# Landing-paced indirect transfers in the first mixture-of-experts layers, with two batches' places computed earlier in the order

## The reference

```python
x = x + gated_attention(layernorm(x))        # groups of 32, cumulative state
x = x + ffn(layernorm(x))                    # "first FFN", same weights as the last
x = x + softmax_attention(layernorm(x))      # 16 heads of 64
x = x + ffn(layernorm(x))

def ffn(x):                                  # E=8 experts, K=2, per batch b
    probs = softmax(x @ Wr); p, e = top_k(probs, 2)
    pos = exclusive_cumsum(one_hot(e))       # place of a token in its expert's queue
    keep = pos < capacity                    # capacity = 160
    buf[e, pos] += x * keep                  # scatter: 2048 rows of 128 into 1280 slots
    y = relu(buf @ W1 + b1) @ W2 + b2        # 128 -> 512 -> 128 by expert
    out = sum_k(y[e, pos] * keep * p)        # gather: two rows for each token
```

## Time and profile before

| | us |
|---|---|
| median of 3 runs | 1488.44 |
| lowest, highest run | 1484.74, 1492.68 |
| span of the profiled execution | 1486.9 |
| busy in it: PE, DVE, ACT, POOL | 1437.6, 1065.3, 917.8, 280.4 |

### The profile page before, as it was taken

How to read it: one execution, slowest core, us unless ns; L and a number is a source line. 1 busy time by engine, 2 the same in 40 slices (tenths; PEclk the granted TensorE clock), 3 DMA queues, 4 the chain that set the end, 5 groups by cost and what they waited for, 6 DMA issues and landing times.

```text
span 1486.9 us, 43341 instructions
## 1 busy us (share of the span) xinstructions
PE 1437.6 (97%) x18426; PEld 1023.7 (69%) x18426; DVE 1065.3 (72%) x2172; ACT 917.8 (62%) x1727; POOL 280.4 (19%) x325
## 2 busy tenths in 40 slices
PE   7999789999999999999999999999999999999996
PEld 6988774566677675667777756577777565677486
DVE  6884037888666678886766788876666887787754
ACT  5774466666666666566666666666666666666542
POOL 4164613013210012130000120400001214000055
PEclk9999999999999999999999999999999999999999
DMA  8501221001110011010000110110101101101002
GB/s 223 196 20 53 68 65 39 22 23 46 30 29 16 16 42 32 23 48 16 17 16 16 41 32 22 35 33 17 30 16 39 32 23 34 34 16 30 1 19 58
DMA packets 44464, 58.30 MB, mean 39 GB/s; under 512 B 8231, under 2 KB 32656, under 8 KB 44144
## 3 DMA queue, kind: packets, MB, share of 16 engines
q1 hardware_dynamic: 35120, 38.27, 9.4%
q0 software_dynamic: 9152, 17.26, 4.4%
HBM read 22.14 MB, written 19.32 MB: 28 GB/s over the span
## 4 chain that ended last, share of the span: by engine, by line
PE 87%; DVE 5%; ACT 3%; issue 2%; another core or an unknown queue 2%; DMA 0%; DVEq 0%; ACTq 0%
PE bank L1153 29%; PE bank L1166 28%; PE bank L1076 6%; PE bank L1081 4%; PE bank L1090 4%; PE bank L412 2%; PE bank L446 2%; PE bank L1308 2%; PE bank L1304 2%; DVE nmx L1188 1%; PE bank L1265 1%; ACT hT L542 1%; PE bank L830 1%; DVE stats L1349 1%
## 5 line engine op out<-in xcount | busy, mean ns | idle before, releaser
L1197 ACT ACTIVATE prob<-bank,nmx 128x1024 f32<-128x1024 f32 x512 | 570.2, 1114 | 420.3 <-DVE nmx L1188 408.5
L1188 DVE TENSOR_REDUCE nmx<-bank 128x1 f32<-128x1024 f32 x512 | 626.2, 1223 | 200.2 <-PE bank L1153 182.3
L1166 PE MATMUL bank<-prob,vsc 64*64 64x512 f32 x4096 | 644.9, 590 | 1.9 <-DVE ctxT L1215 1.4
L1153 PE MATMUL bank<-q,k 64*64 64x512 f32 x2048 | 527.6, 591 | 3.1 <-ACT prob L1197 1.9
L1153 PE MATMUL bank<-q,ks 64*64 64x512 f32 x2048 | 526.3, 590 | 0.0
L1166 PEld LDWEIGHTS bank<-prob,vsc 64*64 64x64 f32 x4096 | 237.3, 133 | 119.4 <-issue 47.1
L1076 PE MATMUL bank<-xT,wqkv_sb 64*64 64x256 f32 (+1 forms) x1560 | 211.7, 434 | 0.0
L1153 PEld LDWEIGHTS bank<-q,ks 64*64 64x64 f32 x2048 | 139.1, 133 | 75.9 <-issue 21.0
L1760 POOL DMA_INDIRECT yg<-yslots,row_ring x64 | 64.9, 1014 | 609.2 <-PE bank L1153 579.8
L1153 PEld LDWEIGHTS bank<-q,k 64*64 64x64 f32 x2048 | 135.3, 133 | 37.6 <-issue 8.6
L1076 PEld LDWEIGHTS bank<-xT,wqkv_sb 64*64 64x64 f32 x1560 | 92.2, 133 | 86.6 <-issue 36.5
(11 more groups left out here) (270 smaller groups left out, 1628.6 us busy)
## 6 DMA issues: line engine op xcount, KB each, us to landing
ks<-k SPq DMA_DIRECT2D x62, 256.0 KB
yslots<-slots_sb SPq DMA_DIRECT2D x7, 640.0 KB, 3.6
slots_sb<-xslots SPq DMA_DIRECT2D x5, 640.0 KB, 4.5
xslots<-xhat_r POOLq DMA_DIRECT2D x5, 512.0 KB, 7.0
yslots<-xhat_r POOLq DMA_DIRECT2D x5, 512.0 KB, 12.3
w_sb<-in_w SPq DMA_DIRECT2D x1, 2048.0 KB, 9.2
wqkv_sb<-in_wqkv SPq DMA_DIRECT2D x1, 2048.0 KB, 19.0
xslots<-xhat_r,row_s POOLq DMA_INDIRECT x112
```

The costliest lines, as they stand in the source:

```text
L1153: ins = nc.tensor.matmul(bank[rows(c), SC[h][n], :], kk[r, cols(2 * j + c, HD)], qst[pi % 2][r, cols(n, HALF)], start=True, stop=True)
L1166: ins = nc.tensor.matmul(bank[rows(h), CX[n], :], vsc[s][rows(r), rows(h)], prob[g % 3][h][rows(r), cols(n, HALF)], start=(j == 0 and firs ...
L1188: nc.vector.tensor_reduce(nmx[:, 2 * s + h:2 * s + h + 1], bank[:, SC[h][0]:SC[h][0] + 2, :], mybir.AxisListType.XY, ALU.max, negate=True) ...
L1197: nc.scalar.activation(prob[g % 3][h][:].rearrange("p (n c) -> p n c", c=HALF), bank[:, SC[h][0]:SC[h][0] + 2, :], ACT.Exp, bias=nmx[:, 2 ...
```

## The change

It does five things, all of them within the first FFNs of batches 0, 1 and 2.

1. The waits on TensorE ahead of the scatters and the gathers (`scatter_in_attention`, `scatter_in_next`, `beside_expert`) are gone. In their place each transfer, from the third of a batch on, waits until the one two in front of it has landed. For this every batch has two semaphores of its own, for even and odd transfers, and so have the gathers.
2. GpSimd's list: 12 scatters of batch 0, the bias of row 3, the places of batch 1 (`place_gpsimd(2)`), the other 4 scatters of batch 0, 16 of batch 1, 16 of batch 2, 16 gathers.
3. The slot numbers of batch 1 get a buffer of their own, row_s2, so `place_gpsimd(2)` doesn't wait for scatters.
4. The counting of batch 2's places (`positions(pe, 3, ...)`) stands ahead of the first expert of batch 0's FFN, no longer behind its third; the wait on its reading (f_kept) stands at expert 2, no longer at expert 5.
5. VectorE writes batch 2's slot numbers itself, as the last step of `place_vector`, once batch 0's scatters have landed; GpSimd's copy (L2065) is gone.

```diff
@@ experts_tensor.up
-                if e == 5 and m == 1:
+                if e == 2 and m == 1:
                     pe.wait_ge(f_kept, 3)
@@ first_batch_tensor.beside
-                if e == 3:
-                    positions(pe, 3, POS_F)
                 if e == E - 1:
-                    pe.wait_ge(f_kept, 3)
                     slots_ahead_tensor(pe, 2, slots2, AHEAD[:2])
@@ place_gpsimd
-            if m > 1:
-                p.wait_ge(f_sc, 256 * (m - 1))
-            nc.gpsimd.tensor_copy(row_s[:], skip[:]).then_inc(f_idx, 1)
+            nc.gpsimd.tensor_copy(rows_to(m)[:], skip[:]).then_inc(f_idx, 1)
@@ place_vector
-            nc.vector.tensor_tensor(skip[:], rowf[:], skip[:], ALU.add).then_inc(f_plc, 1)
+            for done in f_sc[1]:
+                v.wait_ge(done, 128)
+            nc.vector.tensor_tensor(rows_to(m)[:], rowf[:], skip[:], ALU.add).then_inc(f_idx, 1)
@@ scatter
             for c in tiles:
                 k, t = c // T, c % T
+                if c > 1:
+                    hold(p, f_sc[m][c % 2], 16 * (c // 2))
                 nc.gpsimd.indirect_dma_start(...)
@@ gather
-                    beside_expert(p, 11 + 2 * q + k)
                     for t in (2 * q, 2 * q + 1):
+                        n = 4 * q + 2 * k + t % 2
+                        if n > 1:
+                            hold(p, f_gq[(n - 2) // 4][n % 2], 16 * ((n - 2) % 4 // 2 + 1))
                         nc.gpsimd.indirect_dma_start(...)
@@ block.gpsimd
             place_gpsimd(p, step, 1)
-            scatter_in_attention(p, 1, 3)
-            scatter_in_next(p, 1)
+            hold(p, f_idx, 2)
+            scatter(p, 1, range(FIRST))          # FIRST = 12
+            bias_gpsimd(p, 3)
             place_gpsimd(p, step, 2)
-            scatter_in_attention(p, 2)
-            scatter(p, 2, [13, 14, 15])
-            p.wait_ge(f_plc, 1)
-            p.wait_ge(f_sc, 256 * 2)
-            nc.gpsimd.tensor_copy(row_s[:], skip[:]).then_inc(f_idx, 1)
+            scatter(p, 1, range(FIRST, 2 * T))
+            hold(p, f_idx, 3)
+            scatter(p, 2, range(2 * T))
             hold(p, f_idx, 4)
-            for i in range(8):
-                beside_expert(p, 3 + i)
-                scatter(p, 3, [2 * i, 2 * i + 1])
+            scatter(p, 3, range(2 * T))
             gather(p, step, 1, 0)
@@ block.tensor
             pe.wait_ge(f_sub, 4)
+            positions(pe, 3, POS_F)
             experts_tensor(pe, 1, first_batch_tensor(pe), (a_res, 10), following=slots2)
```

More of the change, by code:

```diff
@@ L132, in bass_hybrid @@
         f_kept = sem("f_kept")
-        f_plc = sem("f_plc")
         f_xs, f_ha, f_ya, f_ys = (sem(n) for n in ("f_xs", "f_ha", "f_ya", "f_ys"))
-        f_sc, f_ld, f_st, f_comb = (sem(n) for n in ("f_sc", "f_ld", "f_st", "f_comb"))
+        f_sc = {m: [sem(f"f_sc{m}{i}") for i in range(2)] for m in (1, 2, 3)}
+        f_ld, f_st, f_comb = (sem(n) for n in ("f_ld", "f_st", "f_comb"))
         f_ga = [sem("f_ga0"), sem("f_ga1")]
-        f_gq = [sem(f"f_gq{q}") for q in range(4)]
+        f_gq = [[sem(f"f_gq{q}{i}") for i in range(2)] for q in range(4)]
         f_gb = [sem("f_gb0"), sem("f_gb1")]
@@ L271, in route_norm_scalar @@
             elif k == 2:
-                a.wait_ge(f_sc, 256)
+                for done in f_sc[1]:
+                    a.wait_ge(done, 128)
             for half in range(2):
@@ L615, in kept_vector, with rows_to @@
             nc.vector.tensor_scalar(tmp[:], pos, float(CAP - 1), None, ALU.min).then_inc(f_kept, 1)
+        def rows_to(m):
+            return row_s2 if m == 2 else row_s
         def place_gpsimd(p, step, m):
@@ L656, in first_answers_vector @@
             for q in range(4):
-                v.wait_ge(f_gq[q], 64)
+                for done in f_gq[q]:
+                    v.wait_ge(done, 32)
                 for k in range(2):
@@ L669, in scatter @@
                 k, t = c // T, c % T
-                nc.gpsimd.indirect_dma_start(out=xslots[:, :], out_offset=bass.IndirectOffsetOnAxis(ap=row_s[:, k, t:t + 1], axis=0),
+                if c > 1:
+                    hold(p, f_sc[m][c % 2], 16 * (c // 2))
+                nc.gpsimd.indirect_dma_start(out=xslots[:, :], out_offset=bass.IndirectOffsetOnAxis(ap=rows_to(m)[:, k, t:t + 1], axis=0),
                                              in_=route_rows(m - 1)[:, t, :], in_offset=None,
-                                             bounds_check=B * SLOTS - 1, oob_is_err=False).then_inc(f_sc, 16)
-        def scatter_in_attention(p, m, next_row=None):
-            r = m + 2
-            hold(p, f_idx, m + 1)
-            hold(p, a_vproj, 4 * r + 4)
-            scatter(p, m, [0])
-            hold(p, a_lktr, 2 * r + 2)
-            scatter(p, m, [1])
-            hold(p, a_sq, 2 * r + 2)
-            scatter(p, m, [2])
-            for h in range(2):
-                hold(p, a_sl, 2 * r + h + 1)
-                scatter(p, m, [3 + h])
-            for k in range(2):
-                hold(p, a_kv, 4 * r + 2 * k + 1)
-                scatter(p, m, [5 + k])
-            for k in range(4):
-                hold(p, a_o, 4 * r + k + 1)
-                scatter(p, m, [7 + k])
-                if k == 1 and next_row is not None:
-                    bias_gpsimd(p, next_row)
-            for h in range(2):
-                hold(p, a_out, 2 * r + h + 1)
-                scatter(p, m, [11 + h])
-        def scatter_in_next(p, m):
-            r = m + 3
-            hold(p, a_xproj, 2 * r + 2)
-            scatter(p, m, [13])
-            for k in range(2):
-                hold(p, a_gproj, 4 * r + 2 * k + 2)
-                scatter(p, m, [14 + k])
-        def beside_expert(p, i):
-            hold(p, f_h, E + i + 1)
+                                             bounds_check=B * SLOTS - 1, oob_is_err=False).then_inc(f_sc[m][c % 2], 16)
+        FIRST = 12
         def gather(p, step, m, b):
@@ L1415, in f_norm_vector @@
                 else:
-                    v.wait_ge(f_sc, 256 * (B - 1))
+                    for done in f_sc[B - 1]:
+                        v.wait_ge(done, 128)
                 xhat_vector(v, c0, fb, xhat_r, piece - 5, g_xhat)
@@ L1992, in _ @@
                     store_slots(sp, 1, 0)
-                hold(sp, f_sc, 256 * m)
+                for done in f_sc[m]:
+                    hold(sp, done, 128)
                 hold(sp, f_ld, 16 * m)
```

6 lines of the change are left out of this document (4 added, 2 removed).

## The result

| first comparison, 12 runs each | us |
|---|---|
| before, median (lowest, highest) | 1489.7 (1484.74, 1492.68) |
| after, median (lowest, highest) | 1496.32 (1492.65, 1501.3) |
| after / before, 95% interval | 1.0053 (1.0039 to 1.0068) |
| span of the profiled execution after | 1499.5 |

What follows compares the result with a forecast made beforehand. Late TensorE signals were taken as the bound: 20.1 us to gain, but GpSimd's list then binds, leaving the first projection 13.5 earlier, less 1.5 for the clock: 12.0 off, median 1476.4 us, range 1467 to 1487.

Steps and rivals of the forecast that it cites:

- TensorE's signals: Results arriving 3 to 8 us late in dense transfer runs; without these delays TensorE is ready for batch 0's norm 20.1 earlier.
- The first handover: TensorE's passage from batch 0 to batch 1: 6.6 us without late signals, third expert at 161.0 against 167.16, gain 6.2.
- held back in part: Rival: transfer pairs still delay results passed on at once, costing 10 of the 20.1 us; 1481 us, chance 0.18.
- the third of three scatters starts about 3.0 us behind the first: GpSimd's list with landing waits: 2.2 us landing plus 0.86 restart, so the pitch goes from 1.29 to 1.5 us.
- the 1.5 us that the prediction took off for the clock: Loss from TensorE's steps at half the clock after about 6 us idle, before the first projection.
- The rule of the Trainium skill: GpSimd transfer takes 2.0 us plus bytes at 436 GB/s: 2.15 us for 64 KB, so waits would hold nothing.
- the waits hold nothing: Rival: GpSimd's pitch stays 1.29 us, signals come through anyway, TensorE is the bound; 20.1 off, 1468 us, chance 0.12.
- The cover of 0.9 us ahead of batch 2's slots: Batch 2's slots loaded at 168.6, TensorE wanting them at 169.5; if late, TensorE would stall there instead of at the norm.
- if TensorE waits for batch 2's slots and VectorE's norm in turn: Sign of being wrong; the forecast had a single idle stretch, of about 6 us, ahead of batch 0's norm.
- The slower rival: Rival: 52 transfers in one dense run keep holding back TensorE's signals; 20 us slower, 1508 us, chance 0.17.
- a pitch of 1.5: Spacing of GpSimd's paced scatters, between 1.29 us, which held the signals, and 1.56, which didn't; said to decide the slower case.
- hidden today: GpSimd's transfer list, off the bound before the change, becomes the bound: TensorE ready at 191.8 waits for the norm until 199.

Runs made afterwards that it cites:

- e12: The changed kernel without landing waits between scatters or gathers, on chip 10, where late signals appear: 1524.9 us (one run).
- r1: The kernel before, unchanged, profiled a second time on a chip without late signals: 1463.9 us.
- e6: The changed kernel without landing waits and with row 3's bias behind the eighth scatter: 1457.8 us, 0.9963 of the kernel before.
- r2: The changed kernel, unchanged, on a chip without late signals: 1486.0 us, 1.0156 of the kernel before.

## Why the prediction was wrong

**TensorE's signals: right, for the chip of the first comparison.** The first handover took 6.4 us for 6.6 predicted, the third expert started at 162.62 for 161.0, and from the end of the first wait for slots to the third expert of batch 2 it was 8.45, 1.9 of it for half the clock. In the changed stretch no delay over 1.4 us is left. Beside pairs of transfers with a pause behind each, the signals come through; this is where the change wins, and the "held back in part" rival had too much for it.

**The step that failed: "the third of three scatters starts about 3.0 us behind the first", for the whole list, with gathers at 3.35 for two.** Where nothing runs beside it the number was right (142.91, 145.92: 3.01). But it came from one scatter with nothing beside it, and the list shares the DMA engines with SyncE's five transfers. By batch, first to last transfer, predicted and measured: batch 1, 22.3 and 26.1 (121.13 to 147.23); batch 2, 22.3 and 27.7 (148.50 to 176.16); gathers, 24.8 and 31.2 (178.27 to 209.51). With the pieces between them, 88.4 us for 72.9: 15.5 too little.

The other terms of the 22.6 us by which the first projection missed its 200.6 are smaller. Batch 1's first transfer stood at 121.13 for 116.0: 2.4 of these 5.1 are VectorE's L585, a neighbour that the move of the bias brought and that the sum didn't ask for; 1.8 were there before anything of the change ran (the first scatter of batch 0 started at 81.70 and before at 79.94). From the last gather's start to the whole norm (219.94) it was 0.3 more than predicted, and from there to L1020 3.2 instead of 1.6, since TensorE's steps ran at half the clock behind the idle time of 11.7: the 1.5 us that the prediction took off for the clock in its last line. Together 5.1 + 15.5 + 0.3 + 1.6 = 22.6, within rounding.

**The rule of the Trainium skill** about a transfer alone (2.15 us) agreed with the 2.2 of the quiet stretches. The rival built on it, that the waits hold nothing, failed twice: even in quiet stretches the third transfer starts 3.0 us behind the first and not 2.58, and the landings aren't all quiet ones.

**The cover of 0.9 us ahead of batch 2's slots** was in the prediction as the thin place, and "if TensorE waits for batch 2's slots and VectorE's norm in turn" as what would make it wrong. This came: 6.41 and then 11.70 us.

**The slower rival** didn't come for the change as it stands. Its mechanism came in e12, on a chip that shows late signals and in a run without pauses, where 38 us were lost for its 20. The prediction let a pitch of 1.5 decide, between 1.29 and 1.56. In the quiet stretch from 136.75 to 147.23 the pitch was the predicted 1.5 and no signal was late; whether the pauses do it or the mean pitch is not shown, since no run has one without the other.

**What no row could tell**: that the late signals, 20 us of the sum, hang on the chip and not on the kernel alone. The profile showed them on one chip. On chips without them the same change costs 1.56% in place of 0.53%; there, nothing pays for the landings. The prediction's picture of GpSimd's list as "hidden today" also holds only beside late signals: in r1 it is on the chain already.

**Open.** What makes chip 10 differ from chips 0, 9 and 13, or whether it is the chip at all and not its state at that time, since it was met once; what made the changed kernel's profiled execution 5 us slower than its median; and whether three or four in front, or the old order with waits, keep the signals in time there. No version was measured that beats before on both kinds of chips.

## What to carry to other kernels

A wait for a landing costs what the landing takes at that place, with all other queues' transfers, and not what a quiet one takes: look up what SyncE has under way beside each. If pacing is wanted, leave enough transfers in flight to cover the longest landing: here, against no waits at all, four of 1.28 us cost 0.1% to 0.2%, three 0.8%, two 2.0%. Before winning back a delay that one profile shows, profile the same kernel on a second chip; "another core or an unknown queue" in a program with one core was such a delay. And before setting two profiles' positions against each other, subtract where a step that neither edit touches stands in each: here that moved positions by up to 2.5 us and turned the reading of e6.

## Not expected of the hardware

- One kernel with the same instructions takes 1462 to 1464 us on three chips and 1487 on another; of some 23 us between the two profiles, 13.7 lie ahead of the first projection (213.21 against 199.56) and 7.4 in the last 80 us, in both places with ScalarE waiting for "remote" beside dense runs of GpSimd's transfers.
- On that chip a dense run of GpSimd's indirect transfers makes TensorE's results visible up to 13 us late (132.4 to 145.5) and thins out its issue. In the changed kernel of the first comparison no signal was late beside pairs of transfers with pauses, and one was beside ten without.
- A scatter of 64 KB that lands in 2.3 us alone (2.26 in r2) took 4.4 to 4.9 beside a load of 640 KB and 3.3 to 4.2 beside a store; a gather took 4.3 to 6.1 beside either, once 3.25 (r2, at 189.02).
